# The dense layer's weights are turned and split inside the last batch of the second attention

## The reference, cut to what matters

```python
x = _layernorm(x + _L0_attn_ref(x, Wqkv, Wproj))          # causal attention, 16 heads of 8
x = _layernorm(x + _L0_ffn_ref(x, ...))                   # mixture of experts
x = _layernorm(x + _L1_attn_ref(x, Wq, Wk, Wv))           # attention without a mask
x = _layernorm(x + _L1_ffn_ref(x, w1_w, w1_s, ...))       # the dense layer

def _tlin(x, w, s): return jnp.einsum('bsi,oi->bso', x, w) * s
def _L1_ffn_ref(x, ...):
    h = silu(_tlin(x, w1_w, w1_s)) * _tlin(x, w2_w, w2_s)     # 128 -> 512
    h = gelu(_tlin(h, h1_w, h1_s), approximate=False)         # 512 -> 512
    h = gelu(_tlin(h, h2_w, h2_s), approximate=False)         # 512 -> 512
    return _tlin(h, w3_w, w3_s)                               # 512 -> 128
```

## Time and profile before

| | |
|---|---|
| median of 3 runs | 1450.9 us (1447.1 to 1459.64) |
| the profiled execution | 1459.25 us, of which the span of the trace is 1457.5 us |
| PE busy | 1224.3 us (84%) |
| DVE busy | 923.8 us (63%) |
| ACT busy | 791.2 us (54%) |
| POOL busy | 520.8 us (36%) |
| TensorE's granted clock, mean | 0.917 of full |

### The profile page before, as it was taken

The page is one execution under the profiler, slowest core; times in us unless marked ns, Lnnn a source line. Parts: engine busy times, 40 slices in busy tenths (PEclk is TensorE's granted clock), DMA queues, the critical chain, the costliest instruction groups (busy, mean ns, idle before and its releaser), DMA issues. The chain is left out here.

```text
span 1457.5 us, 28689 instructions
## 1 busy us (share of the span) xinstructions
PE 1224.3 (84%) x10443; PEld 711.0 (49%) x10443; DVE 923.8 (63%) x2838; ACT 791.2 (54%) x1543; POOL 520.8 (36%) x476
## 2 busy tenths in 40 slices
PE   3399888888994976883499999999999959999996
PEld 1245444444443645761144344334343348888885
DVE  3367876678756592537488898888898251345443
ACT  1056655566564833433067677767677635555553
POOL 3225543555322674753303113113110014445452
PEclk9999999999896988995589999999999879999998
DMA  4502212321103103441712122132120000000000
GB/s 103 68 3 46 39 23 31 45 40 27 28 3 112 37 0 95 109 74 20 131 25 31 17 45 32 15 45 31 16 46 2 2 15 8 15 14 15 27 9 15
DMA packets 55948, 53.26 MB, mean 37 GB/s; under 512 B 8000, under 2 KB 38720, under 8 KB 55824
## 3 DMA queue, kind: packets, MB, share of 16 engines
q1 hardware_dynamic: 50528, 47.81, 17.1%
q0 software_dynamic: 3696, 2.76, 1.4%
q10 hardware_dynamic: 1600, 1.05, 0.3%
HBM read 15.74 MB, written 8.06 MB: 16 GB/s over the span
## 5 line engine op out<-in xcount | busy, mean ns | idle before, releaser
L427 ACT ACTIVATE a_prob<-a_ps_s 128x512 f32<-128x512 f32 (+1 forms) x896 | 466.5, 572 | 295.7 <-PE a_ps_s L508 272.5
L594 DVE TENSOR_REDUCE a_mx<-a_ps_m 128x1 f32<-128x512 f32 x512 | 329.2, 685 | 81.9 <-PE a_ps_m L523 80.0
L523 PE MATMUL a_ps_m<-a_kst,a_qst 24*128 24x512 f32 (+3 forms) x1024 | 278.4, 472 | 53.9 <-DMA a_qst<-a_lo_q 38.5
L591 DVE CUSTOM_DVE_ANT_0 a_junk<-a_ps_m,maskw 128x384 f32<-128x384 f32 (+3 forms) x512 | 227.3, 486 | 112.4 <-PE a_ps_m L523 112.0
L545 PE MATMUL a_ps_o<-a_prob,a_vst 128*32 128x256 f32 (+2 forms) x3840 | 279.5, 377 | 14.5 <-ACT a_oT L435 9.9
L508 PE MATMUL a_ps_s<-a_qst,a_kst 25*128 25x512 f32 (+3 forms) x1024 | 247.3, 457 | 22.7 <-ACT a_prob L427 13.7
L508 PEld LDWEIGHTS a_ps_s<-a_qst,a_kst 25*128 25x128 f32 x1024 | 108.9, 190 | 178.5 <-ACT a_prob L427 104.6
L459 PE MATMUL a_ps_s<-a_kst 128*32 128x256 f32 x2000 | 164.6, 403 | 3.6 <-ACT a_prob L427 3.5
L523 PEld LDWEIGHTS a_ps_m<-a_kst,a_qst 24*128 24x128 f32 x1024 | 124.4, 196 | 82.8 <-issue 53.3
L360 POOL TENSOR_SCALAR_AFFINE_SELECT a_prob<-a_prob 128x512 f32<-128x512 f32 x128 | 79.8, 635 | 228.7 <-ACT a_prob L427 228.7
L545 PEld LDWEIGHTS a_ps_o<-a_prob,a_vst 128*32 128x32 f32 x3840 | 85.1, 111 | 114.4 <-issue 62.6
(11 more groups left out here) (292 smaller groups left out, 1929.8 us busy)
## 6 DMA issues: line engine op xcount, KB each, us to landing
a_kst<-a_hi_k SPq DMA_DIRECT2D x128, 64.0 KB
a_qst<-a_hi_q SPq DMA_DIRECT2D x128, 64.0 KB
f_w<-in_L_ffn_W_dram SPq DMA_DIRECT2D x21, 256.0 KB
a_kst<-a_lo_k SPq DMA_DIRECT2D x64, 64.0 KB
a_qst<-a_lo_q SPq DMA_DIRECT2D x64, 64.0 KB
x_tiles<-in_L_attn_x_dram SPq DMA_DIRECT2D x8, 256.0 KB, 4.9
normed_rows_dram<-f_nrm SPq DMA_DIRECT2D x8, 256.0 KB, 2.3
f_hT_hi<-expert_sums_dram SPq DMA_DIRECT2D x4, 512.0 KB, 6.1
```

What stands on the lines that cost most here:

```text
L427: act.activation(prob[k][:, i, 0:w], ps_s[g % SB][:, 0:w], ACT.Exp, scale=float(D) ** -0.5)\
L523: last = pe.matmul(ps_m[g % MB][:, col:col + w], qst[r][lo_row:end, t, P * j:P * j + P], kst[r][lo_row:end, t, 0:w], start=True, stop=True)
L591: ins = dve.tensor_tensor_reduce(junk[g % MB][:, col:col + w], bank[:, col:col + w], maskw[:, T - w:T], 1.0, -3.0e38, ALU.add, ALU.max, out)
L594: ins = dve.reduce_max(out, bank[:, col:col + w], AX.X)
```

## The change

The eleven turns leave the dense layer's block. Each becomes a job ("weight", i) on the bank `ps_x` in the last batch of the second attention. The jobs stand at (group, step) = (1,3) (1,5) (1,7) (1,15) (2,3) (2,5) (2,7) (2,15) (3,3) (3,5) (3,7). PE's part of a job is four transposes as before, ACT's part is the copy to `hi` one unit later, and DVE's part is the subtraction to `lo`, also one unit later, which is what frees the bank. The semaphore `wcast` takes the place of `s_wc`, and `s_wt` and `s_wl` are gone. The tiles `hi` and `lo` are now made by `DenseWeights` and so exist during the attention.

```diff
+    TURNS = [(w, [(0, o) for o in range(FB)]) for w in ("w1", "w2")] + \
+            [(w, [(k, o) for o in range(FB)]) for w in ("h1", "h2") for k in range(FB)] + \
+            [("w3", [(k, 0) for k in range(FB)])]
...
+    def turned(self, part, n):
+        w, blocks = self.TURNS[n]
+        return part[w][:, :, :].rearrange("p k c -> p (k c)") if w == "w3" else part[w][:, blocks[0][0], :]
...
@@ Shapes, not causal
+            spare = [(t, step) for t in range(1, NG) for step in (3, 5, 7, 15)]
+            self.last = {at: ("weight", i) for i, at in enumerate(spare[:len(DenseWeights.TURNS)])}
@@ Shapes.jobs
+        if b == B - 1 and (t, step) in self.last:
+            out.append(self.last[t, step])
@@ attention, ACT's read_out
+                    elif name == "weight":
+                        act.activation(dense.turned(dense.hi, n), ps_x[:, :], ACT.Copy).then_inc(sems.wcast, 1)
+                        return
@@ attention, PE's job
+                    elif name == "weight":
+                        if n == 0:
+                            pe.wait_ge(dense.sem, dense.loads * 16)
+                        w, blocks = dense.TURNS[n]
+                        for i, (k, o) in enumerate(blocks):
+                            last = pe.transpose(ps_x[:, P * i:P * i + P], dense.raw[w][:, o, P * k:P * k + P], ident[:, :])
@@ attention, DVE, for the jobs of sh.behind(n, u, 1)
+                            elif name == "weight":
+                                dve.wait_ge(sems.wcast, m + 1)
+                                dve.tensor_tensor(dense.turned(dense.lo, m), ps_j[place["weight", m][0]][:, :],
+                                                  dense.turned(dense.hi, m).bitcast(F32), ALU.subtract)\
+                                    .then_inc(s_read["weight"], 1)
@@ dense_ffn, ACT
-                for n, (w, blocks) in enumerate(TURNS):
-                    act.wait_ge(s_wt, n + 1)
...
-                    act.activation(dst, src[:, :], ACT.Copy).then_inc(s_wc, 1)
@@ dense_ffn, PE
-                for n, (w, blocks) in enumerate(TURNS):
-                    if n == 0:
-                        pe.wait_ge(s_w, weights.loads * 16)
-                    if n >= 4:
-                        pe.wait_ge(s_wc, n - 3)
-                        pe.wait_ge(s_wl, n - 3)
-                    for i, (k, o) in enumerate(blocks):
-                        last = pe.transpose((ps_a + ps_b)[n % 4][:, P * i:P * i + P], raw[w][:, o, P * k:P * k + P],
-                                            ident[:, :])
-                    last.then_inc(s_wt, 1)
-                pe.wait_ge(s_wc, len(TURNS))
-                pe.wait_ge(s_wl, len(TURNS))
@@ dense_ffn, DVE
-                for n, (w, blocks) in enumerate(TURNS):
-                    dve.wait_ge(s_wc, n + 1)
...
-                    dve.tensor_tensor(lo, (ps_a + ps_b)[n % 4][:, :], hi.bitcast(F32), ALU.subtract).then_inc(s_wl, 1)
```

More of the change, by code:

```diff
@@ L24 @@
 VW = 32
+FF = 512
+FB = FF // P
 EPS = 1e-5
@@ L133, in after, with __init__, load @@
         eng.wait_ge(sem, count)
+class DenseWeights:
+    SHAPES = {"w1": [P, FB, C], "w2": [P, FB, C], "h1": [P, FB, FF], "h2": [P, FB, FF], "w3": [P, 1, FF]}
+    TURNED = {"w1": [P, 1, FF], "w2": [P, 1, FF], "h1": [P, FB, FF], "h2": [P, FB, FF], "w3": [P, FB, C]}
+    TURNS = [(w, [(0, o) for o in range(FB)]) for w in ("w1", "w2")] + \
+            [(w, [(k, o) for o in range(FB)]) for w in ("h1", "h2") for k in range(FB)] + \
+            [("w3", [(k, 0) for k in range(FB)])]
+    def __init__(self, nc, ctx, dram, tag="f1w_"):
+        self.nc, self.dram = nc, dram
+        self.raw = {w: ctx.enter_context(nc.sbuf_tensor(tag + w, shape, F32)) for w, shape in self.SHAPES.items()}
+        self.scale = {w: ctx.enter_context(nc.sbuf_tensor(tag + w + "s", shape[:2], F32))
+                      for w, shape in self.SHAPES.items()}
+        self.hi, self.lo = ({w: ctx.enter_context(nc.sbuf_tensor(tag + w + part, shape, F32R))
+                             for w, shape in self.TURNED.items()} for part in ("_hi", "_lo"))
+        self.sem = ctx.enter_context(nc.semaphore(tag + "loaded"))
+        self.loads = 2 * len(self.SHAPES)
+    def turned(self, part, n):
+        w, blocks = self.TURNS[n]
+        return part[w][:, :, :].rearrange("p k c -> p (k c)") if w == "w3" else part[w][:, blocks[0][0], :]
+    def load(self, sp):
+        for w in self.SHAPES:
+            sp.dma_start(self.raw[w][:, :, :], self.dram[w + "_w"].rearrange("(o p) i -> p o i", p=P)).then_inc(self.sem, 16)
+            with self.nc.allow_non_contiguous_dma(reason="a few hundred scales"):
+                sp.dma_start(self.scale[w][:, :], self.dram[w + "_s"].rearrange("(o p) -> p o", p=P)).then_inc(self.sem, 16)
 class Shapes:
@@ L143, in __init__ @@
             self.maxima = [[(3, 0, T)], [(2, 0, T - P), (0, T - P, P)], [(1, 0, T - 2 * P)]]
+            self.last = {}
             self.values = {9: [(0, 0, 0)], 11: [(0, 0, 1)], 1: [(1, 1, 0), (1, 1, 1)], 3: [(1, 3, 0), (1, 3, 1)],
@@ L207, in sem @@
             return ctx.enter_context(nc.semaphore("a_" + name))
-        small = ("xT", "k", "q", "v", "maxT", "norm", "yT", "proj")
+        small = ("xT", "k", "q", "v", "maxT", "norm", "yT", "proj", "weight")
         self.ones, self.vinit = sem("ones"), sem("vinit")
@@ L226, in __init__ @@
         self.den = sem("den")
+        self.wcast = sem("wcast")
         self.res = sem("res")
@@ L232, in clear, with attention @@
         sp.sem_clear(range(self.ones.num, self.ln.num + 1))
-def attention(nc, sems, x, x_dram, ident, maskw, weights, wproj, cos, sin, tag, ahead=None):
+def attention(nc, sems, x, x_dram, ident, maskw, weights, wproj, cos, sin, tag, dense=None):
     causal = maskw is not None
@@ L317, in _ @@
                 stack(0)
-                if ahead is not None:
-                    ahead(sp)
+                if dense is not None:
+                    dense.load(sp)
                 for b in range(1, B):
@@ L679 @@
 I32 = mybir.dt.int32
-FF = 512
-FB = FF // P
 E = 7
@@ L1489 @@
 RT_STEPS = 61
[L1492 to L1513, removed]
 def dense_ffn(nc, x, ident, weights, out_rows, tag="f1"):
@@ L1529, in dense_ffn @@
         raw, sc, s_w = weights.raw, weights.scale, weights.sem
-        shapes = {"w1": [P, 1, FF], "w2": [P, 1, FF], "h1": [P, FB, FF], "h2": [P, FB, FF], "w3": [P, FB, C]}
-        w_hi = {w: sbuf(w + "_hi", shape, F32R) for w, shape in shapes.items()}
-        w_lo = {w: sbuf(w + "_lo", shape, F32R) for w, shape in shapes.items()}
+        w_hi, w_lo = weights.hi, weights.lo
         half = sbuf("half", [P, FB])
@@ L1554, in dense_ffn @@
         ps_t = psum("ps_t", [P, T])
-        s_wt = sem("wt")
-        s_wc = sem("wc")
-        s_wl = sem("wl")
         s_xl = sem("xl")
@@ L1585, in layer_no @@
             return c * (3 * FB) + FB + f + (0 if n == 0 else FB if last else FB + 2)
-        TURNS = [("w1", [(0, o) for o in range(FB)]), ("w2", [(0, o) for o in range(FB)])] + \
-                [(w, [(k, o) for o in range(FB)]) for w in ("h1", "h2") for k in range(FB)] + \
-                [("w3", [(k, 0) for k in range(FB)])]
         with nc.Block() as block:
@@ L1993, in transformer @@
         weights = DenseWeights(nc, ctx, {n + s: ins["L1_ffn_" + n + s] for n in DenseWeights.SHAPES for s in ("_w", "_s")})
-        attention(nc, sems, x, None, ident, None, heads1, None, cos, sin, "a1_", ahead=weights.load)
+        attention(nc, sems, x, None, ident, None, heads1, None, cos, sin, "a1_", dense=weights)
         dense_ffn(nc, x, ident, weights,
```

## The result

The changed kernel is slightly slower: 1460.49 us against 1450.92 us, medians of 20 runs each. The ratio is 1.0075, 95% interval 1.0051 to 1.0098. That is inside the 1% I called no change and inside the range of 1445 to 1467, and in the forecast direction, but it is 9.6 us and not 5.3, a little over the +9 at which my forecast ended. A repeat beside other kernels (e12) gave 1.0062 (1.0031 to 1.0092). Of the 102 runs of before that were made beside the experiments, two count as slow (1463.81 and 2615.08 us) and are left out of all means.

The account below looks back on a forecast made before the run. PE was taken as the bound, with the turns wholly on the path before. Work 6.6 plus waits 5.6 less gain 6.9 us gave +5.3, so 1456 us against a median of 1450.9, range 1445 to 1467.

Parts of the forecast that it names:

- the +9 at which my forecast ended: Whole run: the forecast was a slowdown of +2 to +9 us, given chance 0.64.
- The gain, 6.9 us: Start of the dense layer: without turns, x can be turned 7.1 us earlier, less 0.2 for half clock; 6.9 us saved.
- Work and waits, 12.2 us: Last three attention groups: eleven transpose jobs on PE cost 6.6 us, waits for the one bank 5.6 us.
- The waits one by one, 0.2, 0.8 and 1.4: Second group from the end: PE waits for the bank before jobs at steps 3, 5 and 7, in us.
- My upper end, 9.9 us of waits: Last three groups: at most 3.3 us of bank waits each, 9.9 in all, making the sum +9.6.
- The clock, "I have left it as it is": Last batch of the attention: PE's clock taken as unchanged, a term of zero, since the waits could go either way.
- What I named as a sign of being wrong: Last batch: no PE idle ahead of steps 5 and 7, or a clock differing by over 5 us.
- My evidence for zero: Attention from 1141 to 1148: PE idle for 1.4 of 7 us, yet keeping full clock.
- The first rival: Clock stays down to the end of the attention after waits at steps 5 and 7: +15 to +17, about 1467; chance 0.13.
- The second rival: Attention: waits are nothing and transposes bring the clock back sooner, -3.7 us, so 1447; chance 0.15.
- The third: Dense layer: late x or first-batch gates leave only 2 of 6.9 us gained; +10, 1461; chance 0.08.

Follow-up runs that it names:

- e12: The changed kernel measured again, unaltered, on the same chip as three other follow-up kernels: 1.0062 of the kernel before, mean 1461.1 us.
- e1: Changed kernel without the eleven turns anywhere; GpSimd fills hi and lo with a constant: 0.9954 of the kernel before, mean 1445.5 us.
- e4: Changed kernel plus unread matmuls ahead of weight jobs, one set at step 5 and two at step 7: 1.0011 of the kernel before, mean 1454.3 us.
- e2: Changed kernel with only TensorE's transposes done; nobody reads the bank, hi and lo are constants: 0.9979 of the kernel before, mean 1448.4 us.
- e10: e5 plus two sets of unread matmuls ahead of each maxima job two units behind a weight job: 0.9979 of the kernel before, mean 1449.7 us.
- e3: Changed kernel without VectorE's subtraction (lo constant), so ScalarE's copy frees the bank: 0.9983 of the kernel before, mean 1449.4 us.
- e11: Changed kernel, but ScalarE copies unrounded into one of three tiles, freeing the bank; VectorE makes hi and lo: 1.001 of the kernel before, mean 1452.7 us.
- e5: Changed kernel with weight jobs spaced, at steps 3, 7 and 15 of all four last-batch groups: 1.0037 of the kernel before, mean 1458.5 us.
- e6: e5 without the set of unread matmuls two units behind each weight job: 1.007 of the kernel before, mean 1461.8 us.

## Why the prediction was right, and where its size was off

- **The gain, 6.9 us**: right. e1 measured 6.7, and the copy of x landed 2.4 us after its issue. The seam kept its length, 7.5 us from the last `norm` to SP's issue in both traces.
- **Work and waits, 12.2 us**: right as a sum, 12.1 us at full clock (e4). The split was not. Transposes alone cost 3 to 4 us and not 6.6, since without waits they also fill idle time (e2). Hence the waits at full clock are some 8 to 9 and not 5.6; two errors cancel, and that part is luck. The waits one by one, 0.2, 0.8 and 1.4, were 0.26, 0.89 and 1.33. In the third group the clock was full in this execution, so they were 0.89 and 1.32 there too, where I had 0.3 and 1.2. My upper end, 9.9 us of waits, gives the +9.6 that was measured; it does so by chance, since it takes 6.6 us for the transposes and nothing for the clock.
- **The clock, "I have left it as it is"**: this is the step that failed. It should have been a term of about 4 us (11 us more at half clock, at 0.32 to 0.41 us each). That idle time is what costs the clock is shown in the means, two ways: filling it (e4, e10) and shortening it (e3, which also leaves DVE's subtraction out) brought the half clock from 237 us to 219, 213 and 219. e11, with waits as short as in e3 and more work for DVE, has 228. What I named as a sign of being wrong, a clock that differs by over 5 us in the last batch, is there in one profiled execution of the changed kernel (30.7 us at half clock against 10.2) and not in the other (10.2). My evidence for zero was one stretch of 7 us with 1.4 us of idle in three short pieces, at full clock. The waits of the change are longer in one piece. The time stayed in the range because the missing term was small beside its width, not because I had priced it.
- **The first rival** (clock down to the end, +15 to +17, 1467) is not the typical case. The changed kernel's first profile comes near it: half clock from 1153.0 to 1180.3 us, 1473.45 us in all. I gave it 0.13; 9 of the 32 runs lie at 1466 us or above. But a long run is no proof of it: e12's profiled one took 1468.95 us with half clock for only 10.2 us of the last batch. The Trainium skill's page "TensorE: Matmul & The Clock Gate", section "A second HAM failure mode: psum-queue depth-cycling", describes a like case: short idle gaps between groups of matmuls while banks are cycled, paid for in clock. The means of e4 and e10 agree with it; the 46.6 us at full clock of e12 show that not every such gap is paid for. It should have been a term of the sum.
- **The second rival** (faster) did not come: the waits were there. A better clock than before, its other half, shows only where they are filled or shortened (213 to 219 us of half clock). **The third** (no gain) is refuted by e1.

## What to carry to other kernels

Work moved under a bound engine is not free even where every other engine has room: price its instructions, and then the wait for the buffer it shares, through every reader up to the last. A wait on TensorE can cost twice, once as time and, in part of the executions, once more as clock; where it can't be removed, filling it with unread matmuls took 7 us off here. Compare such kernels by means of many runs, since two profiles of one kernel differed by 6.8 us in this stretch. Two jobs on one bank should stand further apart than copy plus subtraction, or the first reader should be the one that frees it.

## What was not expected of the hardware

- PE stayed at half clock while busy without a break: 23.9 us of 23.9 in e5, 10.2 of 10.2 in the earlier trace rows.
- The same waits of 0.9 and 1.3 us were followed by half clock twice in one execution, and by none for 46.6 us in another of the same kernel.
- Leaving out unread matmuls beside the transposes raised the half clock from 237 to 255 us (e6); whether for want of them or for the longer waits that came with it is open.
- The granted clock goes with most of the scatter between runs of one kernel: correlation 0.82 over 100 runs of before, 0.32 us of time for each us at half clock.
